# Third attention of a gated four-layer stack: the stacked parts of the queries and keys go through DRAM, and the first tile's maxima are turned in halves

## The chip, the cores and the metric

The kernel runs on one core of a Trainium2 chip. The metric is the device time of one execution in microseconds (us): 1753.15 is the median of three executions (1750.42 to 1754.8). One more execution was recorded by the profiler; the rows below all come from it.

## The reference, cut to what matters

The model has four layers over x of 32 x 64 x 256. Each adds a gated cross-attention-like block and a gated feed-forward block. The change touches only the fourth layer's first block (called the third attention here):

```
scores = einsum('bhtc,bhsc->bhts', rotary(split_heads(Wq x + bq)), rotary(split_heads(Wk c + bk))) / sqrt(8)
out = einsum('bhts,bhsc->bhtc', softmax(scores), split_heads(Wv c + bv))
x = x + tanh(g_xattn[3]) * (Wo out + bo)
```

x is read here as 32 batches of 64 channels by 256 positions; there are 8 heads of 8 channels. So each batch and head has a 256 x 256 matrix of scores over only 8 channels.

## The kernel before, in words

The eight blocks of the model run one after another on all engines. Each engine has its own program, written by hand, in loops over blocks of four tiles; engines wait for one another by semaphores. PE is TensorE, DVE VectorE, ACT ScalarE, POOL GpSimd, SP the sync engine that issues transfers.

In the third attention a tile is two batches: 128 partitions are 2 batches (k) x 64 channels, and there are 16 tiles. The scores must be as exact as float32, but their matmuls run in bf16. So a rotated query or key row is split by POOL into three bf16 parts that sum to it (`split`, lines 2160 to 2163: four operations for the queries, z = 0, and four for the keys, z = 1). The product is then the sum over six pairs of parts, `PAIRS3`. To have these six sums in one matmul, the parts are stacked: 6 pairs x 8 channels are 48 rows per batch, `MROW`. In the parts a partition is a channel of a head (64 per batch); in the stacks `qS` and `kS` a partition is a pair and one of 8 channels, and the heads lie beside one another (8 x 256 elements). That change of layout is done by transfers within the on-chip memory: SP issues at line 2131, for each z, batch and pair, one transfer of 64 rows of 512 bytes. That is 24 issues per tile, which all add to `stack_in`.

With the stacks there, PE makes scores twice. `largest` (line 1956) has queries on the partitions, and DVE takes row maxima (line 2224, 16 per tile). The negated maxima are split in two bf16 parts (`split_largest`, lines 2234 and 2235, per half of the heads), turned by PE (line 1965), copied by ACT (line 2075) and sent by ACT (line 2078, two transfers per half) as rows 48 and 49 of `qS`. `scores` (line 1977) then makes the transposed scores over 50 rows, with the maxima already taken off; ACT exponentiates (line 2098) and PE multiplies by the values (line 1991).

What sets the order: tile n does for each head h the scores and exponentials of tile n, one small step, the value product of the head before, and two units of `largest` of tile n + 1. The small steps are, for h = 0 to 7, those in `STEPS3` = (0, 7, 2, 1, 3, 5, 4, 6). Step 0 projects the queries of tile n + 2 (line 1942), step 2 its keys; DVE rotates them (lines 2203 and 2208), POOL splits them, SP stacks them. So a stack has about one tile of time from its projection to its first use: PE waits for `stack_in` of tile n + 1 at the first `largest` of tile n. POOL's split of a tile waits until the whole stack before it has landed, since there is one buffer of parts. In the second tile of each block of four DVE also makes the next block's layer norm (`normalise`, 21 small operations and eight larger ones). The last of the SP work is line 2338, the output of 2048 KB to DRAM.

The first tile has no tile before it: its stacks, all 16 maxima units, the split and the turn of both halves' maxima stand before the first scores.

Of the kernel before, what the change touches and what calls it, by code (L numbers as in the profile page):

```python
# [5 lines left out]
BF16 = mybir.dt.bfloat16  # L6
# [6 lines left out]
P = 128  # L13
BATCH, SEQ, DIM = 32, 64, 256
# [18 lines left out]
H3, D3 = 8, 8  # L33
# [27 lines left out]
def flamingo_kernel(nc, a, out):  # L61
    ctx = ExitStack()
    with ctx:
# [3 lines left out]
        def sem(name):  # L67
            return ctx.enter_context(nc.semaphore(name))
# [54 lines left out]
        def updated(ph, b):  # L123

            return BLOCKS * ph + b + 1
# [215 lines left out]
        z, at = part(work, at, [P, 2, BTOK])  # L341
# [844 lines left out]
        def bf_bank(i):  # L1186
            return bank[i].bitcast(BF16)
# [626 lines left out]
        C3 = DIM  # L1814
        PAIRS3 = ((0, 0), (0, 1), (0, 2), (1, 0), (1, 1), (2, 0))

        MROW = len(PAIRS3) * D3
        HALF = H3 // 2
        VW3 = SEQ
# [13 lines left out]
        parts3, at = part(work, at, [P, 3, 2, C3], BF16)  # L1833
# [18 lines left out]
        assert at <= 5632, at  # L1852
        vv3 = (vv0, vv1)

        a3_in = sem("a3_in")
        bd_zero = sem("bd_zero")
        vv_clear = sem("vv_clear")
        cs_ready = sem("cs_ready")
# [6 lines left out]
        stack_in = sem("stack_in")  # L1865
# [45 lines left out]
        def has_step(n, step):  # L1911
            if not isinstance(n, int):
                return True
            ahead = (2, None, 2, None, None, 1, 1, 0)[step]
            return n >= 1 if ahead is None else n + ahead < TILES
# [10 lines left out]
        def stack_rows(k, rows):  # L1926
            return slice(k * SEQ, k * SEQ + rows)

        def attn3_tensor(pe, ph):
# [16 lines left out]
            def largest(m, i, units):  # L1946

                if units[0] == 0:
                    pe.wait_ge(stack_in, 16 * STACK_DMAS * (m + 1))
                for u in units:  # L1950
                    k, tc, hp = u % 2, u // 2 % 2, u // 4
                    rows = stack_rows(k, MROW)
                    if u >= 2 or not isinstance(m, int) or m >= 1:
                        pe.wait_ge(mx_read, 16 * m + u - 1)
                    for h in range(2):
                        ins = nc.tensor.matmul(bank[u % 2][:, h * C3:(h + 1) * C3],  # L1956
                                               qS[rows, i, 2 * hp + h, tc * P:(tc + 1) * P], kS[rows, i, 2 * hp + h, :],
                                               start=True, stop=True)
                    ins.then_inc(s1_done, 1)

            def turn_largest(m, half, used):
                pe.wait_ge(m_ready, 2 * m + half + 1)
                pe.wait_ge(misc_read, used)
                for tc in range(2):
                    ins = nc.tensor.transpose(bf_bank(7)[0:4 * HALF, tc * P:(tc + 1) * P],
                                              mm3[:, half, tc, :, :, :].rearrange("p k s h -> p (k s h)"), ident_h[:, :])
                ins.then_inc(m_turned, 1)

            def scores(n, i, h):
# [4 lines left out]
                for sc_ in range(2):  # L1974
                    for k in range(2):
                        rows = stack_rows(k, MROW + 2)
                        ins = nc.tensor.matmul(bank[2 + 2 * (h % 2) + k][:, sc_ * C3:(sc_ + 1) * C3],  # L1977
# [76 lines left out]
            project(0, 0, 2, 2)  # L2054
            project(1, 1, 0, 3)
            project(1, 1, 1, 4)
            largest(0, 0, range(16))
            turn_largest(0, 0, 5)
            for t in range(BT):
                tile_(0, t)  # L2060
            with pe.Fori(1, BLOCKS - 1) as b:
# [8 lines left out]
        def attn3_scalar(act, link, ph):  # L2070
            def largest(m, i, half, used):
# [5 lines left out]
                for k in range(2):  # L2077
                    act.dma_start(qS[k * SEQ + MROW:k * SEQ + MROW + 2, i, half * HALF:(half + 1) * HALF, :],
                                  mT3[2 * k * HALF:2 * (k + 1) * HALF, half, :]).then_inc(mrow_in[half], 16)
# [36 lines left out]
            outputs(TILES - 1)  # L2116
            turned(TILES - 1)

        STACK_DMAS = 4 * len(PAIRS3)

        def attn3_dmas(sp, ph):
            def stack(m, i):

                for z, stacks in enumerate((qS, kS)):
                    sp.wait_ge(parts_ready, 2 * m + z + 1)
                    for k in range(2):
                        for c, parts in enumerate(PAIRS3):
                            rows = slice(k * SEQ + c * D3, k * SEQ + (c + 1) * D3)  # L2130
                            sp.dma_start(stacks[rows, i, :, :],  # L2131
                                         parts3[k * SEQ:(k + 1) * SEQ, parts[z], z, :]).then_inc(stack_in, 16)

            def tile_(b, t):
                n = BT * b + t
                if has_step(n, 0):
                    stack(n + 2, (t + 2) % BT)

            sp.wait_ge(vv_clear, 1)
            stack(0, 0)  # L2140
            stack(1, 1)
            for t in range(BT):
                tile_(0, t)
            with sp.Fori(1, BLOCKS - 1) as b:
                for t in range(BT):
                    tile_(b, t)
            for t in range(BT):
                tile_(BLOCKS - 1, t)

        def attn3_gpsimd(pool, link, ph):  # L2150
            def split(m):

                if not isinstance(m, int) or m >= 1:

                    pool.wait_ge(stack_in, 16 * STACK_DMAS * m)
                one = ones[:, 0:1].broadcast_to([P, C3])
                for z in range(2):
                    pool.wait_ge(rot_ready, 2 * m + z + 1)
                    p = [parts3[:, s, z, :] for s in range(3)]
                    link(nc.gpsimd.tensor_tensor(p[0], rot3[:, z, :], one, ALU.mult))  # L2160
                    link(nc.gpsimd.tensor_tensor(rest3[:, z, :], rot3[:, z, :], p[0], ALU.subtract))
                    link(nc.gpsimd.tensor_tensor(p[1], rest3[:, z, :], one, ALU.mult))
                    nc.gpsimd.tensor_tensor(p[2], rest3[:, z, :], p[1], ALU.subtract).then_inc(parts_ready, 1)

            def contexts(b):
                nc.gpsimd.tensor_tensor(cs3, ctx_nat[:, bass.ds(BT * b, BT), :],
                                        ones[:, 0:1].unsqueeze(2).broadcast_to([P, BT, C3]), ALU.mult).then_inc(cs_ready, 1)

            def tile_(b, t):
                n = BT * b + t  # L2170
                if has_step(n, 0):
                    split(n + 2)
                if t == BT - 2 and has_step(n, 0):
                    pool.wait_ge(p3_v, BT * b + BT)
                    contexts(b + 1)

            pool.wait_ge(x_done, updated(ph, 0))
            pool.wait_ge(ctx_in, 16)
            contexts(0)
            split(0)  # L2180
            split(1)
            clear_values(link, 1).then_inc(vv_clear, 1)
            for t in range(BT):
                tile_(0, t)
            with pool.Fori(1, BLOCKS - 1) as b:
                link.enter(b - 1, 6 * BT)
                for t in range(BT):
                    tile_(b, t)
            link.leave(BLOCKS - 2)
            for t in range(BT):  # L2190
                tile_(BLOCKS - 1, t)

        def attn3_vector(dve, link, ph):
# [26 lines left out]
            def largest(m, units):  # L2220
                for u in units:
                    k, tc, hp = u % 2, u // 2 % 2, u // 4
                    dve.wait_ge(s1_done, 16 * m + u + 1)
                    nc.vector.tensor_reduce(out=mx3[:, tc, k, 2 * hp:2 * hp + 2],  # L2224
                                            in_=bank[u % 2].rearrange("p (h s) -> p h s", h=2), axis=AX,
                                            op=ALU.max).then_inc(mx_read, 1)

            def split_largest(m, half):

                dve.wait_ge(mx_read, 16 * m + 8 * half + 8)  # L2230
                if not isinstance(m, int) or m >= 1:
                    dve.wait_ge(m_turned, 2 * m + half - 1)
                mx, mm = mx3[:, :, :, half * HALF:(half + 1) * HALF], mm3[:, half, :, :, :, :]
                link(nc.vector.tensor_scalar(mm[:, :, :, 0, :], mx, -1.0, None, ALU.mult))
                nc.vector.scalar_tensor_tensor(out=mm[:, :, :, 1, :], in0=mx, scalar=-1.0, in1=mm[:, :, :, 0, :],
                                               op0=ALU.mult, op1=ALU.subtract).then_inc(m_ready, 1)
                dve.wait_ge(m_ready, 2 * m + half + 1)
# [55 lines left out]
            values(0, 0)  # L2293
            rotate(1, 0, p3_q)
            rotate(1, 1, p3_k)
            largest(0, range(16))
            split_largest(0, 0)
            split_largest(0, 1)
            for t in range(BT):
                tile_(0, t)  # L2300
            with dve.Fori(1, BLOCKS - 1) as b:
# [183 lines left out]
```

## Time and profile before

| | us |
|---|---|
| median of the executions shown | 1753.15 |
| the profiled execution | 1745.52 |
| its span, first to last instruction | 1743.7 |
| third attention, first issue of a stack (1178.18) to the last tile's first `largest` (1528.14) | 349.96 |

Busy in the span: PE 1290.4 us (74%), DVE 1066.2 (61%), ACT 455.2 (26%), POOL 306.9 (18%). "SPq" is SP's queue of transfer issues, and its time is no busy time of the table. The share of an engine over the whole span says little on this change: the eight stages have different limits, and only the stage from 1178 us on is touched. The granted TensorE clock (PEclk) is in parts of full speed.

### The profile page before, as it was taken

How to read it: one execution, taken by the hardware profiler on the slowest of the kernel's cores; microseconds unless marked ns; L12 is line 12 of the kernel's file. 1: busy time of each engine (PE TensorE's matmuls, PEld its weight loads, DVE VectorE, ACT ScalarE, POOL GpSimd, SP SyncE). 2: the span in 40 equal slices, each digit the busy share in tenths (PEclk: the TensorE clock that was granted, in tenths of full speed). 3: DMA queues.
4: the chain of work that ended last, by engine and by line, in shares of the span. 5: the costliest groups of instructions: out<-in, count | busy, mean ns of one | idle time of the engine just before them, and what ended most of it. 6: DMA issues, size and time to landing. Idle time of an engine off the chain costs nothing.

```text
span 1743.7 us, 20441 instructions
## 1 busy us (share of the span) xinstructions
PE 1290.4 (74%) x6664; PEld 725.4 (42%) x6670; DVE 1066.2 (61%) x2575; ACT 455.2 (26%) x632; POOL 306.9 (18%) x287
## 2 busy tenths in 40 slices
PE   0011899999979989957767445545888888899997
PEld 0010544444434456635544222222444444455554
DVE  8988434454353356557767788874778777742222
ACT  1124222222113133322222122211444434351110
POOL 2111000000013500022344222233132222200000
PEclk9995899999989999988898566675899999999999
DMA  9000000002000010011110000001111111100001
GB/s 301 12 13 11 1 0 0 0 0 100 0 19 0 0 61 0 1 25 25 24 24 0 19 1 0 0 0 37 38 38 39 39 37 37 38 2 1 0 0 48
DMA packets 65554, 43.16 MB, mean 25 GB/s; under 512 B 25040, under 2 KB 61776, under 8 KB 65232
## 3 DMA queue, kind: packets, MB, share of 16 engines
q1 hardware_dynamic: 64848, 42.09, 8.4%
q8 instruction: 33, 0.54, 0.1%
q14 instruction: 33, 0.27, 0.1%
q10 hardware_dynamic: 640, 0.26, 0.1%
HBM read 27.39 MB, written 2.10 MB: 17 GB/s over the span
## 4 chain that ended last, share of the span: by engine, by line
PE 49%; DVE 19%; issue 12%; SPq 9%; POOL 5%; ACT 2%; DMA 2%; DVEq 0%; POOLq 0%; ACTq 0%
SPq L2131 9%; PE banks L1004 6%; PE banks L406 5%; PE banks L623 5%; PE banks L402 5%; PE banks L837 3%; PE banks L1011 3%; POOL sb_work L1429 3%; PE banks L829 3%; PE banks L413 2%; PE banks L417 2%; DMA sb_work<-sb_work 2%; PE banks L1991 2%; DVE sb_work L317 2%; PE banks L1622 1%
## 5 line engine op out<-in xcount | busy, mean ns | idle before, releaser
L2224 DVE TENSOR_REDUCE sb_work<-banks 128x2 f32<-128x512 f32 x256 | 164.2, 685 | 68.5 <-PE banks L1956 64.3
L2098 ACT ACTIVATE sb_work<-banks 128x1024 f32<-128x1024 f32 x128 | 130.7, 1023 | 178.4 <-PE banks L1977 178.2
L523 DVE TENSOR_TENSOR sb_work<-sb_work,banks 128x512 f32<-128x512 f32 x72 | 49.4, 686 | 123.6 <-ACT sb_work L490 123.6
L1004 PE MATMUL banks<-sb_work,sb_shelf 128*128 128x512 f32 x256 | 114.4, 592 | 0.0
L1429 POOL TENSOR_TENSOR sb_work<-sb_work,sb_consts 128x512 f32<-128x512 f32 x64 | 66.4, 1067 | 265.7 <-ACT sb_work L1377 232.9
L1956 PE MATMUL banks<-sb_work 48*128 48x256 bf16 x512 | 65.4, 297 | 51.8 <-DMA sb_work<-sb_work 40.1
L406 PE MATMUL banks<-sb_work,sb_shelf 128*128 128x512 f32 (+1 forms) x192 | 92.2, 630 | 8.6 <-DVE sb_work L566 8.6
L623 PE MATMUL banks<-sb_work,sb_ctx_nat 128*64 128x512 f32 (+15 forms) x512 | 89.8, 510 | 7.8 <-DVE sb_work L685 7.8
L490 ACT ACTIVATE sb_work<-banks 128x512 f32<-128x512 f32 x72 | 42.9, 596 | 181.6 <-PE banks L402 116.2
L1083 DVE TENSOR_TENSOR sb_work<-sb_work,banks 128x512 f32<-128x512 f32 x32 | 22.0, 688 | 109.9 <-ACT sb_work L1069 109.9
L980 POOL TENSOR_TENSOR sb_late<-sb_w2n 128x1024 f32<-128x1024 f32 x10 | 22.7, 2268 | 371.6 <-DVE sb_work L677 370.9
L402 PE MATMUL banks<-sb_work,sb_shelf 128*128 128x512 f32 (+1 forms) x192 | 84.9, 593 | 0.0
L1991 PE MATMUL banks<-sb_work,sb_late 128*64 128x256 f32 x512 | 76.9, 425 | 0.2
L230 PE MATMUL banks<-sb_ident,sb_work 128*128 128x128 f32 x32 | 7.9, 427 | 92.6 <-DVE sb_work L319 92.6
L1991 PE MATMUL banks<-sb_work,sb_shelf 128*64 128x256 f32 x512 | 70.3, 396 | 0.0
L1004 PEld LDWEIGHTS banks<-sb_work,sb_shelf 128*128 128x128 f32 x256 | 48.6, 190 | 49.2 <-issue 47.8
L837 PE MATMUL banks<-sb_wpr,sb_work 128*128 128x256 f32 x256 | 61.6, 387 | 6.9 <-DVE sb_work L916 6.9
L1956 PEld LDWEIGHTS banks<-sb_work 48*128 48x128 bf16 x512 | 18.4, 96 | 114.1 <-issue 44.1
L829 PE MATMUL banks<-sb_work,sb_wgu 128*128 128x512 f16 x256 | 61.8, 388 | 2.5 <-DVE sb_work L898 2.5
L1639 PE MATMUL banks<-sb_ident_h,sb_work 128*128 128x128 bf16 x128 | 16.2, 305 | 62.9 <-DVE sb_work L1760 62.9
L623 PEld LDWEIGHTS banks<-sb_work,sb_ctx_nat 128*64 128x64 f32 x512 | 36.6, 136 | 60.1 <-issue 44.4
L1719 POOL TENSOR_TENSOR sb_work<-sb_work 128x512 f32<-128x512 f32 x32 | 40.2, 1266 | 118.5 <-ACT sb_work L1684 118.4
(285 smaller groups left out, 2599.4 us busy)
## 6 DMA issues: line engine op xcount, KB each, us to landing
sb_work<-sb_work SPq DMA_DIRECT2D x384, 32.0 KB
sb_work<-ctx_t SPq DMA_DIRECT2D x16, 256.0 KB, 4.4
sb_work<-ctx_t SPq DMA_DIRECT2D x4, 512.0 KB, 3.7
sb_ctx_nat<-ctx SPq DMA_DIRECT2D x1, 2048.0 KB, 11.0
sb_raw<-wguT SPq DMA_DIRECT2D x1, 2048.0 KB, 15.4
out<-sb_x SPq DMA_DIRECT2D x1, 2048.0 KB, 7.5
sb_x<-x SPq DMA_DIRECT2D x1, 1536.0 KB, 10.7
sb_raw<-wpT SPq DMA_DIRECT2D x1, 1024.0 KB, 13.4
```

Of the source, the lines that this page charges most:

```text
L402: ins = nc.tensor.matmul(dst[0:ms, :], w[:, c, m0:m0 + ms], moe_xT[:, c, :], start=c == 0, stop=c == KC - 1, skip_group_check=True)
L406: ins = nc.tensor.matmul(dst[0:ms, :], w[:, m0:m0 + ms], zz[:, k, :], start=False, stop=True, skip_group_check=True)
L623: ins = nc.tensor.matmul(o, ctx_nat[:, tap, g * SEQ:(g + 1) * SEQ], xg[:, g, :, l0 + 1 + 2 * tap:SEQ + 1 + 2 * tap], start=tap == TILES - ...
L829: ins = nc.tensor.matmul(bank[2 * (m % 2) + half], wgu[:, c, half * FF1 + m * P:half * FF1 + (m + 1) * P], xs[:, c, :], start=c == 0 and n ...
L837: ins = nc.tensor.matmul(bank[4 + t // 2][:, (t % 2) * DIM:(t % 2 + 1) * DIM], h1[:, m % 4, t * P:(t + 1) * P], wpr[:, m, :], start=m == 0 ...
L1004: ins = nc.tensor.matmul(bank[2 * (m % 2) + half], w[:, c, m * P:(m + 1) * P], xT3[:, c, :], start=c == 0, stop=c == KC - 1)
L1429: ins = nc.gpsimd.tensor_tensor(km_[:, hf, k, :, :], keys.unsqueeze(1).broadcast_to([P, 8, SEQ]), hm2.unsqueeze(2).broadcast_to([P, 8, SEQ ...
L1956: ins = nc.tensor.matmul(bank[u % 2][:, h * C3:(h + 1) * C3], qS[rows, i, 2 * hp + h, tc * P:(tc + 1) * P], kS[rows, i, 2 * hp + h, :], st ...
L1991: ins = nc.tensor.matmul(bank[6][k * SEQ:(k + 1) * SEQ, u * C3:(u + 1) * C3], vv3[j][:, sc_, 2 * k + u, a_ * VW3:(a_ + 1) * VW3], pt3[:, h ...
L2098: nc.scalar.activation(pt3[:, h % 2, :, :], o, ACT.Exp).then_inc(exp3, 1)
L2131: sp.dma_start(stacks[rows, i, :, :], parts3[k * SEQ:(k + 1) * SEQ, parts[z], z, :]).then_inc(stack_in, 16)
L2224: nc.vector.tensor_reduce(out=mx3[:, tc, k, 2 * hp:2 * hp + 2], in_=bank[u % 2].rearrange("p (h s) -> p h s", h=2), axis=AX, op=ALU.max).t ...
```

## The change

Each batch of three bf16 parts is written to a DRAM tensor `scratch`, already repeated as the pairs need it: `RUNS3` says that pairs 0 to 2 are written by one transfer, pairs 3 and 4 by a second, pair 5 by a third. For the queries one part is repeated over the pairs of a run; for the keys the parts 0 to n - 1 follow one another. Then SP waits until the three have landed (`parts_out`), and reads the stack back with one transfer per batch: 48 rows of 4096 bytes. So a tile has 10 issues, 6 out and 4 back, and two new waits on SP. POOL waits for `parts_out` too before it overwrites the parts.

Apart from that, the first tile's maxima are cut in two halves of 8 units: DVE splits the first half's after 8 units, and PE turns them before it goes on with the second 8.

```
+        RUNS3 = ((0, 3, 0), (3, 2, 1), (5, 1, 2))
...
+        scratch = nc.dram_tensor("scratch", (2, len(PAIRS3), 2, D3, H3, C3), BF16, kind="Internal").ap()
...
-            largest(0, 0, range(16))
+            largest(0, 0, range(8))
             turn_largest(0, 0, 5)
+            largest(0, 0, range(8, 16))
...
-        STACK_DMAS = 4 * len(PAIRS3)
+        STACK_DMAS = 4
...
                 for z, stacks in enumerate((qS, kS)):
                     sp.wait_ge(parts_ready, 2 * m + z + 1)
+                    for c0, n, s in RUNS3:
+                        src = parts3[:, s:s + 1, 0, :] if z == 0 else parts3[:, 0:n, 1, :]
+                        sp.dma_start(scratch[z, c0:c0 + n].rearrange("c k d h t -> (k d h) c t"),
+                                     src.broadcast_to([P, n, C3])).then_inc(parts_out, 16)
+                    sp.wait_ge(parts_out, 96 * m + 48 * z + 48)
                     for k in range(2):
-                        for c, parts in enumerate(PAIRS3):
-                            rows = slice(k * SEQ + c * D3, k * SEQ + (c + 1) * D3)
-                            sp.dma_start(stacks[rows, i, :, :],
-                                         parts3[k * SEQ:(k + 1) * SEQ, parts[z], z, :]).then_inc(stack_in, 16)
+                        sp.dma_start(stacks[k * SEQ:k * SEQ + MROW, i, :, :],
+                                     scratch[z, :, k].rearrange("c d h t -> c d (h t)")).then_inc(stack_in, 16)
...
+                    pool.wait_ge(parts_out, 96 * m)
                     pool.wait_ge(stack_in, 16 * STACK_DMAS * m)
...
-            largest(0, range(16))
-            split_largest(0, 0)
-            split_largest(0, 1)
+            for half in range(2):
+                largest(0, range(8 * half, 8 * half + 8))
+                split_largest(0, half)
```

On SP, the stage before began with the constants of this attention and then the stacks of the first six tiles in a row (144 issues; `REGISTER_ALU` and `ISA` are the loop's counters and waits):

```order
L1884 DMA sb_late<-w3T 64x64 x12
L1886 DMA sb_late<-b 64x5 x2
L1887 DMA sb_late<-rope 128x1024
L1889 DMA sb_late<-bv 128x64 x2
L2131 DMA sb_work<-sb_work 8x8x256 x144
```

Now the same place reads, for the two halves z of the first tile:

```order
L1893 DMA sb_late<-bv 128x64 x2
L2135 DMA scratch<-sb_work 128x3x256
L2135 DMA scratch<-sb_work 128x2x256
L2135 DMA scratch<-sb_work 128x256
L2139 DMA sb_work<-scratch 48x1x2048 x2
L2135 DMA scratch<-sb_work 128x3x256
L2135 DMA scratch<-sb_work 128x2x256
L2135 DMA scratch<-sb_work 128x256
L2139 DMA sb_work<-scratch 48x1x2048 x2
```

Twelve issues of 8 x 8 x 256 elements became three of 128 rows, a wait, and two of 48 rows.

On DVE, the maxima of the first tile stood before as one row of 16 with both halves' splits behind (2203 and 2208 are rotations, 2224 the maxima, 2234 and 2235 the split):

```order
L2203 SCALAR_TENSOR_TENSOR sb_work<-banks,sb_late 128x256 x2
L2208 TENSOR_TENSOR sb_work<-sb_work 128x256
L2224 TENSOR_REDUCE sb_work<-banks 128x2 x16
L2234 TENSOR_SCALAR sb_work<-sb_work 128x4x4
L2235 SCALAR_TENSOR_TENSOR sb_work<-sb_work 128x4x4
L2234 TENSOR_SCALAR sb_work<-sb_work 128x4x4
L2235 SCALAR_TENSOR_TENSOR sb_work<-sb_work 128x4x4
```

Now (lines 2233, 2243 and 2244 are the old 2224, 2234 and 2235):

```order
L2212 SCALAR_TENSOR_TENSOR sb_work<-banks,sb_late 128x256 x2
L2217 TENSOR_TENSOR sb_work<-sb_work 128x256
L2233 TENSOR_REDUCE sb_work<-banks 128x2 x8
L2243 TENSOR_SCALAR sb_work<-sb_work 128x4x4
L2244 SCALAR_TENSOR_TENSOR sb_work<-sb_work 128x4x4
L2233 TENSOR_REDUCE sb_work<-banks 128x2 x8
L2243 TENSOR_SCALAR sb_work<-sb_work 128x4x4
L2244 SCALAR_TENSOR_TENSOR sb_work<-sb_work 128x4x4
```

The first split moved ahead of the second eight maxima; every later tile is as it was.

## Rows read from the trace of the kernel before

**Rows 1.** The page, part 4: shares of the chain, by line.
```profile
SPq L2131 9%; PE banks L1004 6%; PE banks L406 5%; PE banks L623 5%; PE banks L402 5%; PE banks L837 3%; PE banks L1011 3%; POOL sb_work L1429 3%; PE banks L829 3%; PE banks L413 2%; PE banks L417 2%; DMA sb_work<-sb_work 2%; PE banks L1991 2%; DVE sb_work L317 2%; PE banks L1622 1%
```

**Rows 2.** Waits from 1178 to 1545 us: total us, times, longest.
```profile
POOL sb_work L2160 <- DMA sb_work<-sb_work: 81.0, 8, 14.8
...
PE banks L1956 <- DMA sb_work<-sb_work: 40.1, 12, 11.6
```

**Rows 3.** Busy us (x) of PE, PEld, DVE, ACT, POOL; PEclk; DMA; tile by tile.
```profile
1236.58:1262.06 25.48, 22.48 (x152) 11.54 (x153) 20.48 (x63) 8.97 (x11) 5.13 (x8) 0.80 0.13 33
...
1284.34:1305.12 20.78, 19.72 (x153) 10.40 (x153) 15.31 (x35) 9.56 (x12) 5.12 (x8) 0.88 0.16 39
...
1325.80:1349.34 23.54, 19.96 (x152) 10.42 (x153) 20.18 (x63) 8.97 (x11) 5.13 (x8) 0.93 0.14 35
...
1414.63:1439.50 24.87, 21.29 (x153) 10.97 (x154) 20.21 (x62) 8.97 (x11) 5.13 (x8) 0.86 0.13 33
...
1504.09:1528.14 24.05, 20.01 (x148) 9.75 (x149) 19.33 (x59) 8.85 (x11) 5.12 (x8) 0.86 0.14 34
sum 312.32, PE 267.91 PEld 140.60 DVE 236.93 ACT 132.77 POOL 77.50; mean PE 19.14 PEld 10.04 DVE 16.92 ACT 9.48 POOL 5.54
```

**Rows 4.** Timeline of PE, 1303 to 1326: start, us, line, [idle <-releaser].
```profile
1325.80 0.40 PE L1956 MATMUL banks<-sb_work 48*128 48x256 bf16 x4 [3.12 <-DMA sb_work<-sb_work]
```

**Rows 5.** Timeline of PE, 1365 to 1372.
```profile
1365.19 0.39 PE L1977 MATMUL banks<-sb_work 50*128 50x256 bf16 x4
...
1370.88 0.40 PE L1956 MATMUL banks<-sb_work 48*128 48x256 bf16 x4 [3.23 <-DMA sb_work<-sb_work]
```

**Rows 6.** Timeline of PE, 1284 to 1306, after a long wait.
```profile
1284.34 0.61 PE L1956 MATMUL banks<-sb_work 48*128 48x256 bf16 x4 [4.15 <-DMA sb_work<-sb_work]
...
1285.62 1.98 PE L1991 MATMUL banks<-sb_work,sb_late 128*64 128x256 f32 x8
...
1289.98 1.08 PE L1991 MATMUL banks<-sb_work,sb_late 128*64 128x256 f32 x8
...
1305.12 0.40 PE L1956 MATMUL banks<-sb_work 48*128 48x256 bf16 x4 [0.99 <-DMA sb_work<-sb_work]
```

**Rows 7.** Timeline of POOL, 1345 to 1372: the split of one tile.
```profile
1350.47 0.61 POOL L2160 TENSOR_TENSOR sb_work<-sb_work,sb_ones 128x256 bf16<-128x256 f32 x1 [13.83 <-DVE sb_work L2208]
...
1352.60 0.67 POOL L2163 TENSOR_TENSOR sb_work<-sb_work 128x256 bf16<-128x256 f32 x1
1355.11 0.61 POOL L2160 TENSOR_TENSOR sb_work<-sb_work,sb_ones 128x256 bf16<-128x256 f32 x1 [1.85 <-DVE sb_work L2208]
```

**Rows 8.** Line 2131 on SP: ns min/median/max of one issue.
```profile
L2131 SPq DMA_DIRECT2D sb_work<-sb_work x384: 599/613/1784, 1178.2 to 1523.7; - x192
```

**Rows 9.** Chain of waits, 1330 to 1350: the last landing of a stack.
```profile
1343.92 2.28 DMA sb_work<-sb_work
```

**Rows 10.** DMA issues: count, KB each, median us from issue to landing.
```profile
out<-sb_x SPq DMA_DIRECT2D x1, 2048.0 KB, 7.5
...
sb_late<-rope SPq DMA_DIRECT2D x1, 512.0 KB, 3.7
...
sb_late<-w3T SPq DMA_DIRECT2D x12, 16.0 KB, 2.0
```

**Rows 11.** Line 2338 on SP: ns of its issue.
```profile
L2338 SPq DMA_DIRECT2D out<-sb_x x1: 402/402/402, 1735.8 to 1735.8; - x1
```

**Rows 12.** Chain of waits, 1170 to 1216: the first tile.
```profile
1178.18 0.80 SPq L2131
...
1195.68 0.66 PE banks L1956 x4
...
1206.14 1.29 DVE sb_work L2224 x2
...
1209.90 2.10 DMA sb_work<-sb_work
```

**Rows 13.** Timeline of ACT, 1345 to 1372: the maxima's rows.
```profile
1360.76 1.31 ACTq L2078 DMA_DIRECT2D sb_work<-sb_work  x2
```

More of the change, by code:

```diff
@@ L1853, in flamingo_kernel @@
         vv3 = (vv0, vv1)
+        scratch = nc.dram_tensor("scratch", (2, len(PAIRS3), 2, D3, H3, C3), BF16, kind="Internal").ap()
         a3_in = sem("a3_in")
+        parts_out = sem("parts_out")
         bd_zero = sem("bd_zero")
```

## The prediction, made before the changed kernel was run

> **What bounds the kernel now.** Read first, in the page, the shares of the chain that ended last by line: SP's queue at line 2131, the issues of the stacks, has 9% of the span, more than any line of an engine [rows 1]. That is one line with 384 issues, so ask next who waited for it. The list of waits between 1178 and 1545 us gives two: PE's line 1956, the first `largest` of a tile, waited 40.1 us in 12 waits, and POOL's line 2160 81.0 us in 8 [rows 2]. Then cut the stage tile by tile, from each first `largest` to the next, and read the length, DVE's busy time and the clock of each [rows 3]. The 14 tiles from 1215.82 to 1528.14 take 312.32 us. Four of them hold a layer norm and take 25.48, 23.54, 24.87 and 24.05, together 97.94; the ten others take 214.38, so 21.44 each.
>
> What would a tile take if no stack were late? The timeline of PE tells it. The tile from 1305.12 ends at 1325.80, after 3.12 us of waiting for the transfer: 20.68 - 3.12 = 17.56 [rows 4]. The one from 1349.34 ends at 1370.88 after 3.23: 18.31 [rows 3, 5]. The tile from 1284.34 waited only 0.99 at its end, yet took 20.78 [rows 3, 6]. Look at its start: PE had been idle for 4.15 us, and the value product of eight matmuls that follows takes 1.98 instead of 1.08; it is at 1.08 again at 1289.98. The granted clock of that tile is 0.88 against 1.00 where there was no slow stretch. So a late stack costs twice: the wait, and some matmuls at 1.2 GHz instead of 2.4 after it. That is 0.9 from the product, 0.2 from each of four groups of scores (0.61 against 0.40 [rows 4, 6]) and about 0.5 from a projection, 2.2 us, my estimate; without it and the wait the tile takes 20.78 - 0.99 - 2.2 = 17.6. The layer-norm tile from 1325.80 ends with no stack late and has 20.18 us of DVE in 23.54 [rows 3]; it too began after a wait of 3.12 [rows 4], at clock 0.93, and 0.07 of its time is 1.6. It would take 21.9, and there DVE is the bound.
>
> Why the stack is late: POOL needs 1352.60 + 0.67 - 1350.47 = 2.80 us for one z [rows 7], 24 issues at 0.656 from start to start (0.613 and a gap) [rows 8] are 15.7, and the last one lands 2.28 after it is issued [rows 9]. Since POOL overwrites the parts only after that, the sum, 20.8 us, is the shortest time from stack to stack. It is longer than 17.6 or 18.3.
>
> **The change, part by part.**
>
> Removed: per tile 24 issues, 15.7 us of SP, on the path in the ten short tiles, hidden in the four with a layer norm.
>
> Added, per z: three issues of 128 rows. The trace has no such transfer out of the parts. The issue of the output took 0.40 [rows 11], a stack issue 0.61 [rows 8]; three cost 1.3 to 2.0. Then a wait for the landing in DRAM, call it W, from the end of the issue. From below: the output, 2048 KB, lands 7.5 after its issue, and the small load w3T of 16 KB 2.0 after its issue, of which the issue itself is 0.6 [rows 10], so 1.4 and at the very least 1.2. From above: the stack's own landing of 2.28 [rows 9], plus 0.6 for a third transfer that is still behind the first two: 2.9. I take W = 2.0, nearer the stack's landing, since the source is the same. Then two issues at 0.656, and for the last z a landing R of 2 x 192 KB in rows of 4096 bytes. The rope table, 512 KB in such rows, lands in 3.7 against 2.0 for 16 KB [rows 10]: 1.7 us for 128 rows, 0.21 per row if 16 engines take eight each. R is 1.4 + 0.6 = 2.0 if the 96 rows spread as widely; if they went over only six engines, 16 rows each, 3.4 us of data begun 0.65 before, it would be 4.1. I take 3.0, the middle.
>
> A rule that speaks against this change bears on R. The Trainium skill, page "DMA: Bandwidth & Descriptors", section on why a DMA increments its semaphore by 16, says that a transfer runs on the largest number of engines up to 16 that divides both sides' slowest dimension; 48 rows on one side and 6 pairs on the other would give 6. No row here shows it. By it the sum below would have R = 4.1, 1.1 us more per stack.
>
> The wait also blocks: SP is in order, so the keys' three issues stand behind the queries' landing in DRAM. Nothing else is queued there; the output comes after the stage. The first z's POOL work starts 1.13 after the tile's start (1350.47 - 1349.34) [rows 3, 7]. The chain from a tile's first `largest` to the next stack is then 1.13 + 2.80 + 2 x (3 issues + W + 2 issues) + R. With 5 issues at 0.656 (3.3) and W = 2.0 it is 3.93 + 10.6 + 3.0 = 17.5. The keys' own way is not longer: their parts are ready at 1355.11 + 2.80 - 1349.34 = 8.6, and SP is free for them at 3.93 + 5.3 = 9.2. With all at the lower ends (2.6 + 1.2 twice, R = 2.0) it is 13.5; with all at the upper (3.3 + 2.9 twice, R = 4.1) 20.4.
>
> 17.5 is as long as the 17.6 of the short tiles and under the 18.3, so the stack is just in time and PE's own order becomes the bound. What is late next: in the layer-norm tile DVE, elsewhere PE with its value products and DVE's maxima in turn. The 14 tiles are four with a norm at 21.9 (87.6), four like the one from 1349.34 at 18.3 (73.2) and six at 17.6 (105.6), together 266.4: 45.9 less than 312.3. As the stack is only just in time I leave 5 us in for short waits: -41.
>
> Start of the stage: the first issue is at 1178.18, the first `largest` at 1195.68 [rows 12]. Now the first stack is there at 1178.2 + 10.6 + 3.0 = 1191.8. The second follows POOL: 1191.9 + 2.8 + 10.6 + 3.0 = 1208.3, where the second tile's `largest` ran at 1215.82.
>
> Maxima in halves: from 1195.68 the 16 units took until 1207.4 [rows 12] at half clock, 0.73 each; with the split, turn and ACT's rows, landing 2.10 after 1209.90 [rows 12], the first scores came at 1212.0 and the next `largest` 3.8 later. Uncut, that would be 1191.8 + 16.3 + 3.8 = 1211.9, later than the stack's 1208.3. Cut, the rows of the first half travel while the second 8 units run: these start about 1.2 late, for PE waits for the split and turn before them, and end at 1191.8 + 11.8 + 1.2 = 1204.8, so 1204.8 + 3.8 = 1208.6. The two parts of the change need each other here. Together 1215.8 - 1208.6 = 7. POOL's added wait for `parts_out` is covered by that for `stack_in`, which comes later: nothing.
>
> Sum: -41 - 7 = -48. On the profiled execution's 1745.52 that gives 1697.5. That execution is 7.6 below the median of 1753.15; on the median, which is what will be measured, 1705.
>
> **The rivals.**
>
> The round trip through DRAM binds. With W and R at the upper ends a stack is there after 20.4. The short tiles take 20.4 (ten times 1.0 less), the four others lose about 0.5 each, the start gains 1 to 2: -14, 1739. For it: nothing in the trace goes out and comes back, and two waits stand in a row on SP for each z. Against it: all landings of small transfers are 1.3 to 2.3 after the issue [rows 9, 10].
>
> Slower than before: the same chain, each landing dearer than any row. It decides where the chain passes the 21.44 of the ten tiles now: 3.93 + 6.6 + 2W + R = 21.44, so 2W + R = 10.9. With W = 4.5 (DRAM behind 128 x 3 small rows) and R = 5 the chain is 24.5; ten tiles lose 3.1, the four others nothing, and the second stack comes 6.5 later than now (7.8 for each z, 2.8 for POOL, 5 for R, twice over): +37, 1790. Against it speaks the output, which writes 2048 KB in 7.5 all told [rows 10]; a W of 4.5 for 64 KB behind 320 KB has no like.
>
> The maxima's rows come late. ACT sends them from 1360.76 for 1.31 us, and they land 2.10 later [rows 12, 13], at 1364.2; the scores that need them run at 1365.19 [rows 5]. One us of slack. The read-back falls into this stretch with 4096-byte rows on the same engines, where there were 512-byte ones. If that holds the rows for 3 us, each tile waits 2: 28 of the gain go, 1733. Against it: they need only a few packets, and the transfers use 0.16 of the engines' time.
>
> **How the numbers follow.** The forecast, 1705, has 0.62; its own range is 1690 to 1722, from all waits gone to 1 us left per tile. DRAM binding has 0.20, the late maxima 0.11, slower 0.07. The range 1688 to 1742 takes in the second and third and leaves out the slower case and what lies below. Runs of this kernel tell 0.3%, 5 us, from no change: 1748 to 1758. Of the DRAM case a quarter lies in that or beyond: faster 0.88, same 0.05, slower 0.07.
>
> **What would show it.** SP's line 2135 with issues of 0.4 to 0.65 and a wait behind each three of about 2 us; landings of line 2139 of 2 to 4 us. PE's waits of the first `largest` for the transfer should fall from 40.1 us to under 10, the 14 tiles from 312.3 to about 271 with the norm tiles near 22, the clock in them near 1.0, POOL's line 2160 waiting for DVE rather than for the transfer. The first `largest` should start near 1191.8 and the second tile's near 1208.6. I am wrong if tiles without a norm stay above 20 us; then the chain of waits names SP and the scratch transfers (DRAM), or `scores` waiting for ACT's rows (the third rival).

## The result, and the profile after

| | before | changed |
|---|---|---|
| median, us | 1749.74 (6 runs, 1742.34 to 1754.8) | 1734.79 (6 runs, 1726.74 to 1737.55) |
| ratio | | 0.9914, 95% interval 0.9893 to 0.9935 |
| profiled execution, us | 1745.52 | 1737.16 |
| its span | 1743.7 | 1735.4 |
| 14 tiles, first maxima of the second tile to those of the last | 312.32 | 302.60 |
| POOL's first split to the second tile's first maxima | 1215.82 - 1175.24 = 40.6 | 1216.31 - 1176.95 = 39.4 |

The changed kernel is 0.86% faster, 15 us. I had forecast 48 us. The profiled pair differs by 8.4 us only: the profiled execution of the kernel before is among the shorter of its kind, that of the changed kernel among the longer. Of the 8.4, 9.7 are in the tiles and 1.2 at the start, and the stage begins 1.7 later.

The shares of the chain, in the page of the changed kernel (line numbers are up to 9 higher than before):

```profile
PE banks L1004 6%; PE banks L623 5%; PE banks L406 5%; PE banks L402 5%; DMA sb_work<-scratch 4%; DMA scratch<-sb_work 3%; PE banks L837 3%; PE banks L1011 3%; POOL sb_work L1429 3%; PE banks L829 3%; PE banks L413 2%; PE banks L417 2%; DVE sb_work L317 2%; PE banks L1622 1%; PE banks L1995 1%
```

SP's queue is gone from the head of the list of [rows 1]. Two kinds of landing came instead: the read back with 4% and the write out with 3%. The list of waits from 1178 to 1545 us answers [rows 2]:

```profile
POOL sb_work L2169 <- DMA sb_work<-scratch: 95.0, 10, 14.5
...
PE banks L1960 <- DMA sb_work<-scratch: 31.3, 11, 11.3
```

PE's wait for the stack fell from 40.1 to 31.3 us only; POOL's grew from 81.0 to 95.0. So the stack is still late. Tile by tile, with the columns of [rows 3]:

```profile
1235.42:1257.87 22.45, 19.46 (x152) 10.14 (x153) 20.40 (x63) 8.98 (x11) 5.14 (x8) 0.92 0.24 72
...
1278.92:1298.45 19.53, 17.52 (x152) 9.59 (x153) 15.54 (x35) 9.57 (x12) 5.14 (x8) 1.00 0.27 82
1298.45:1318.76 20.31, 17.41 (x153) 9.45 (x153) 15.55 (x35) 9.57 (x12) 5.15 (x8) 0.99 0.28 81
1318.76:1345.69 26.93, 22.62 (x153) 11.33 (x153) 20.30 (x62) 8.97 (x11) 5.14 (x8) 0.82 0.20 60
...
1412.10:1435.70 23.60, 20.36 (x155) 10.52 (x154) 20.20 (x63) 9.58 (x12) 5.14 (x8) 0.89 0.23 68
...
1494.50:1518.91 24.41, 21.51 (x148) 10.76 (x149) 19.57 (x59) 8.86 (x11) 5.14 (x8) 0.79 0.23 66
sum 302.60, PE 265.88 PEld 139.54 DVE 237.03 ACT 132.89 POOL 77.68; mean PE 18.99 PEld 9.97 DVE 16.93 ACT 9.49 POOL 5.55
```

The ten tiles without a norm fell from 21.44 to 20.5 on average ((302.60 - 22.45 - 26.93 - 23.60 - 24.41) / 10), and to 19.9 without the one of 26.43; not to 17.6 or 18.3. The tiles with a norm are near what they were (97.94 before, 97.39 now).

The tile from 1385.67 took 26.43 us, and 22.43 before. It holds the step from one round of the loop to the next, at which VectorE does nothing for 3.40 us and waits for nothing that the profile shows. That step is no work of the change: before it took 3.23. New in this tile are a wait of 1.96 us for the rows of the maxima (shown below, with the third rival) and slow stretches: the granted clock is 0.84 against 1.00 before.

Where is the time between the parts and the stack? In the chain of waits of the first tile (start us, us, what; a landing counts from the end of the last issue):

```profile
1180.86 1.80 DMA scratch<-sb_work
...
1185.44 5.06 DMA scratch<-sb_work
...
1191.28 5.70 DMA sb_work<-scratch
```

The first z lands in DRAM after 1.80 us, as forecast (W = 2.0). The second z needs 5.06. The last landing of the read back, R, needs 5.70, where I had taken 3.0 and had an upper end of 4.1. A later tile shows the same:

```profile
1267.20 5.93 DMA scratch<-sb_work
...
1273.92 4.96 DMA sb_work<-scratch
```

The issues were no surprise. A write took 0.48 us in the median and a read 0.73; the writes, as ns min/median/max:

```profile
L2135 SPq DMA_DIRECT2D scratch<-sb_work x96: 369/480/1729, 1179.9 to 1506.1; - x96
```

What the transfer engines move during the read back of the first keys (40 slices of 0.175 us from 1190.5 us):

```profile
GB/s 0 0 0 0 0 0 0 0 70 70 70 47 70 94 70 140 164 140 140 164 140 117 140 187 117 140 23 23 47 23 47 0 0 0 0 0 0 0 0 0
```

There is no slice over 187 GB/s, and the best stretch stays near 140 to 164. The output of the kernel before moves 2048 KB in 7.5 us [rows 10], 280 GB/s, waits at both ends included. That made me suspect that only a part of the engines carries the read back.

### The profile page after: what moved, and what is told of

The parts are those of the page before. It is cut to its first block, busy times and chain, and to the rows that moved or that the text cites. A ratio compares the mean times of both kernels' runs of the same rounds, so it can differ in the third digit from the quotient of the medians.

```text
span 1735.4 us, 20241 instructions
## 1 busy us (share of the span) xinstructions
PE 1288.0 (74%) x6664; PEld 724.3 (42%) x6670; DVE 1071.7 (62%) x2575; ACT 455.5 (26%) x632; POOL 307.6 (18%) x287
## 4 chain that ended last, share of the span: by engine, by line
PE 48%; DVE 19%; issue 13%; DMA 8%; POOL 6%; ACT 2%; SPq 2%; DVEq 0%; POOLq 0%; ACTq 0%
PE banks L1004 6%; PE banks L623 5%; PE banks L406 5%; PE banks L402 5%; DMA sb_work<-scratch 4%; DMA scratch<-sb_work 3%; PE banks L837 3%; PE banks L1011 3%; POOL sb_work L1429 3%; PE banks L829 3%; PE banks L413 2%; PE banks L417 2%; DVE sb_work L317 2%; PE banks L1622 1%; PE banks L1995 1%
## 5 line engine op out<-in xcount | busy, mean ns | idle before, releaser
L1960 PE MATMUL banks<-sb_work 48*128 48x256 bf16 x512 | 64.3, 295 | 41.2 <-DMA sb_work<-scratch 31.3
L1960 PEld LDWEIGHTS banks<-sb_work 48*128 48x128 bf16 x512 | 18.3, 96 | 102.3 <-DVE sb_work L2233 38.5
```

## The experiments

Each kernel was timed against the kernel before on the same chip, and the ratios are to it. One execution of each also left a trace.

**1. Only DRAM, without the halves.** The changed kernel with the first tile's maxima whole:

```
-            largest(0, 0, range(8))
+            largest(0, 0, range(16))
             turn_largest(0, 0, 5)
-            largest(0, 0, range(8, 16))
```

(and the same on VectorE.)

> The parts go through DRAM as in the changed kernel, the first tile's maxima are not cut in halves. If the halves are worth little because the second tile's stack (from the chain of waits of the changed kernel, 1216.3 us) sets the next step: 0 to 2 us slower than the changed kernel (scores of the first tile start some 4 us later, but the second stack comes when it comes). If the halves carry the gain: back to the time of the kernel before, 15 us slower than the changed one.

Measured: 1733.58 us, ratio 0.9913 (0.9882 to 0.9945), against 0.9914 with the halves. No difference that can be told: the gain that the medians show is from DRAM. The timeline of PE, with the first maxima, the first scores and then the second tile's first maxima, shows in this kernel

```profile
1200.48 0.61 PE L1960 MATMUL banks<-sb_work 48*128 48x256 bf16 x4 [10.65 <-DMA sb_work<-scratch]
...
1219.88 0.61 PE L1981 MATMUL banks<-sb_work 50*128 50x256 bf16 x4 [6.93 <-DMA sb_work<-sb_work]
...
1222.42 0.61 PE L1960 MATMUL banks<-sb_work 48*128 48x256 bf16 x4
```

and in the changed kernel

```profile
1197.03 0.61 PE L1960 MATMUL banks<-sb_work 48*128 48x256 bf16 x4 [11.28 <-DMA sb_work<-scratch]
...
1210.39 0.70 PE L1981 MATMUL banks<-sb_work 50*128 50x256 bf16 x4
...
1216.31 0.61 PE L1960 MATMUL banks<-sb_work 48*128 48x256 bf16 x4 [3.21 <-DMA sb_work<-scratch]
```

With the halves PE gets to the scores sooner and then waits 3.21 us for the stack. From the first maxima to the second tile's it is 19.28 us with the halves and 21.94 without, 2.7 us more, which is too little for these medians to tell. Before it was 20.14, so the way through DRAM alone makes this place slower. The scores wait 6.93 us here, for the rows of the maxima: these land 4.88 us after their issue, where it was 2.10 before [rows 12]. They are issued while SP issues the read back of the second stack, so the likely cause is that the two share transfer engines; that was not tried apart.

```profile
1214.95 4.88 DMA sb_work<-sb_work
```

**2. Eight engines for the read back.** The order of two letters in the changed kernel, so that the outermost dimension in DRAM is the 8 channels and not the 6 pairs:

```
-                                     scratch[z, :, k].rearrange("c d h t -> c d (h t)")
+                                     scratch[z, :, k].rearrange("c d h t -> d c (h t)")
```

Queries and keys are both stacked so, and a sum over 48 rows does not mind their order.

> Only the order of the 48 rows of a stack is changed, (channel, pair) instead of (pair, channel), for queries and keys alike; the read back then has 8 and not 6 as its outermost dimension on the DRAM side. Theory 1 (the 96 rows of 4096 bytes of a read back run over only as many transfer engines as divide both sides' outermost dimension, six): now eight engines, 12 rows each instead of 16; the last landing falls from about 5.6 us to 4.6 to 5.0, and the keys' landing in DRAM, which stands behind the queries' read back, from about 4.7 to 4; a stack comes 1 to 1.7 us sooner, ten short tiles gain that: 8 to 15 us faster than the changed kernel. Theory 2 (the landing is long because DRAM answers late, whatever the engines): no change within 4 us, landing stays at 5.6.

Measured: 1711.84 us, ratio 0.9783 (0.9758 to 0.9808): 23 us below the changed kernel, and the best of all. The same place in the chain:

```profile
1266.89 4.23 DMA scratch<-sb_work
...
1271.85 4.25 DMA sb_work<-scratch
```

The write went from 5.93 to 4.23, the last landing from 4.96 to 4.25 (5.70 to 4.24 in the first tile). The tiles:

```profile
1276.14:1293.96 17.82, 17.53 (x152) 9.61 (x153) 15.12 (x35) 9.29 (x13) 5.13 (x8) 1.00 0.31 90
...
sum 281.97, PE 259.42 PEld 137.36 DVE 237.22 ACT 132.54 POOL 77.50; mean PE 18.53 PEld 9.81 DVE 16.94 ACT 9.47 POOL 5.54
```

They sum to 281.97 instead of 302.60, and the 23 us are more than the 8 to 15 that I expected. The chain of a stack got 2.4 us shorter, and a stack that comes within the 18.4 us or so of a tile costs nothing: from the second tile on no wait of PE for a stack is over 0.75 us.

**3. All engines for the read back, at the price of more issues.** DRAM laid out per batch, so that both sides of a read are 48 adjoining rows:

```
+        scratch = nc.dram_tensor("scratch", (2, 2, len(PAIRS3), D3, H3, C3), BF16, kind="Internal").ap()
...
+                        for k in range(2):
+                            own = parts3[k * SEQ:(k + 1) * SEQ]
+                            src = own[:, s:s + 1, 0, :] if z == 0 else own[:, 0:n, 1, :]
+                            sp.dma_start(scratch[z, k, c0:c0 + n].rearrange("c d h t -> (d h) c t"),
+                                         src.broadcast_to([SEQ, n, C3])).then_inc(parts_out, 16)
...
+                                     scratch[z, k].rearrange("c d h t -> (c d) (h t)")).then_inc(stack_in, 16)
```

> The DRAM tensor is laid out per batch, so a stack of one batch is 48 adjoining rows on both sides (16 divides both); in exchange each write out is cut in two of 64 rows, six issues per z instead of three. Theory 1: all 16 engines read, 6 rows each: the last landing falls from about 5.6 to 2.5 to 3.2 us and the keys' landing in DRAM to about 2; the three more issues per z cost 1.4 us of SP each. The stack comes 1 to 2.5 us sooner, 10 to 25 us faster than the changed kernel. Theory 2: landing stays near 5.6, and the more issues make it 10 to 25 us slower than the changed kernel.

Measured: 1729.79 us, ratio 0.9883 (0.9859 to 0.9908), 5 us below the changed kernel where I had expected 10 to 25, and with intervals that overlap; 14 tiles in 295.75. The chain and the rate (slices of 0.125 us from 1193.5):

```profile
1273.86 1.89 DMA scratch<-sb_work
...
1276.12 3.50 DMA sb_work<-scratch
```

```profile
GB/s 0 49 168 45 0 0 0 0 0 0 0 0 0 0 164 164 66 164 492 295 361 426 164 295 131 164 229 33 0 0 0 0 0 0 0 0 0 0 0 0
```

The landing is 3.50 and the keys' write 1.89, and the rate reaches 492 GB/s in a slice. The landings are as theory 1 has them, or a little longer, and theory 2 fails. The time gained is small, as the six issues of 0.61 us per z take it back (three took 1.43 us in the changed kernel). The Trainium skill says how the engines are chosen (page "DMA: Bandwidth & Descriptors", section on why a DMA increments its semaphore by 16): the largest number up to 16 that divides both outermost dimensions. By it the three kernels use 6, 8 and 16. The traces agree: 5.70, 4.24 and 3.54 us in the first tile. No row names an engine, but the packets count them. The two reads of 48 rows are 96 packets of 4096 bytes, and beside them stand short ones:

```profile
DMA packets 108, 0.39 MB, mean 56 GB/s; under 512 B 12, under 2 KB 12, under 8 KB 108
DMA packets 112, 0.39 MB, mean 77 GB/s; under 512 B 16, under 2 KB 16, under 8 KB 112
DMA packets 208, 0.43 MB, mean 85 GB/s; under 512 B 48, under 2 KB 112, under 8 KB 208
```

The first line is the changed kernel (1190.5 to 1197.5 us), the second run 2 (1194.9 to 1200): 12 and 16 short packets for two transfers, 6 and 8 each. In the third, run 3 (1193.5 to 1198.5), the last write of 64 rows falls into the stretch, so it is 48 for three transfers, 16 each. These are the three numbers of the rule, if each engine adds one short packet per transfer. The order of the rows in DRAM also differs among the three kernels; what that adds was not tried apart.

**4. The floor.** The kernel before with one pair stacked of six, and ones in the rest:

```
-        STACK_DMAS = 4 * len(PAIRS3)
+        STACK_DMAS = 4
...
-                        for c, parts in enumerate(PAIRS3):
+                        for c, parts in enumerate(PAIRS3[:1]):
...
+            link(nc.vector.memset(qS, 1.0))
```

> The kernel before, but with only the first of the six pairs stacked (4 issues per tile instead of 24; the other 40 rows of every stack hold ones, set once by VectorE at the start of the stage, about 5 us). So no stack can be late. If my floor of a tile holds (17.6 to 18.3 us, 21.9 with a layer norm), the 14 tiles take 264 to 272 us instead of 312, no matmul in them runs at half clock for lack of work, and the whole is 40 to 50 us below the kernel before. Rival: the tiles are bound by PE and VectorE near 20 us anyway, and the 14 tiles take 290 or more: then the changed kernel could not have gained more than it did.

Measured: 1715.16 us, ratio 0.9817 (0.9786 to 0.9849). The tiles:

```profile
1253.64:1271.70 18.06, 17.87 (x155) 9.72 (x154) 15.53 (x37) 9.52 (x12) 7.03 (x9) 1.00 0.04 9
...
1308.24:1332.62 24.38, 20.27 (x155) 10.41 (x153) 21.14 (x65) 9.52 (x12) 5.13 (x8) 0.93 0.03 7
1332.62:1351.02 18.40, 17.86 (x155) 9.54 (x154) 15.47 (x36) 9.52 (x12) 7.03 (x9) 1.00 0.04 9
...
sum 286.71, PE 263.64 PEld 139.10 DVE 237.75 ACT 132.31 POOL 77.53; mean PE 18.83 PEld 9.94 DVE 16.98 ACT 9.45 POOL 5.54
```

The 14 tiles take 286.71, neither the 264 to 272 of the forecast nor quite the 290 of the rival. Most short tiles take 18.06 to 18.48 at full clock; one of 22.21 is again that at the step between rounds of the loop. The four with a norm take 98.3, as long as in the kernel before, though no stack is late. The timeline of PE in the second of them says why:

```profile
1323.44 0.39 PE L1956 MATMUL banks<-sb_work 48*128 48x256 bf16 x2 [2.09 <-DVE sb_work L2225]
...
1325.20 1.87 PE L1991 MATMUL banks<-sb_work,sb_late 128*64 128x256 f32 x8
```

PE waits for VectorE twice, 1.14 and then 2.09 us, and after that runs a value product at 1.87 instead of 1.08. So a tile with a norm can have a slow stretch without any late stack, behind the norm's own wait; here all four have one. But such a wait does not always bring one. In the kernel before, the tile with a norm from 1325.80 has the same wait of 2.09, and the product behind it takes 1.08; its slow stretch stands at its start, behind the wait of 3.12 for the stack:

```profile
1326.56 1.66 PE L1991 MATMUL banks<-sb_work,sb_late 128*64 128x256 f32 x8
...
1341.45 0.39 PE L1956 MATMUL banks<-sb_work 48*128 48x256 bf16 x2 [2.09 <-DVE sb_work L2224]
...
1343.22 1.08 PE L1991 MATMUL banks<-sb_work,sb_late 128*64 128x256 f32 x8
```

And one of the four in run 2 has no slow stretch at all:

```profile
1235.05:1257.55 22.50, 18.59 (x154) 9.90 (x152) 21.17 (x66) 9.51 (x12) 5.13 (x8) 1.00 0.24 72
```

So 286.71 is no floor to the last us either: run 2, in which all six pairs are still stacked, takes 281.97. Its ten tiles without a norm take 188.22 against 188.40 here; the whole difference is in the four with a norm, 93.75 against 98.31. The medians of the two runs, 1711.84 and 1715.16, cannot be told apart. The floor of the 14 tiles lies at 282 to 287.

**5. Both writes before either read.** The changed kernel, with SP's first wait moved behind the writes of both z:

```
-                    sp.wait_ge(parts_out, 96 * m + 48 * z + 48)
+                sp.wait_ge(parts_out, 96 * m + 96)
+                for z, stacks in enumerate((qS, kS)):
```

> As the changed kernel, but SP writes out the queries' and the keys' parts before it reads back either stack; the keys' writes so no longer stand behind the queries' read back on the same transfer engines. If that queue is why the keys' landing in DRAM takes 4 to 5 us against 1.8 of the queries', it falls to about 2 for both. The four read backs then stand in a row (32 rows on each of six engines): the last lands 8 to 9 us after its issue instead of 5.5. Sum within 2 us per stack of the changed kernel, so within 15 us of it. If the keys' landing stays at 4 to 5 us, something else delays it.

Measured: 1740.51 us, ratio 0.9966 (0.9944 to 0.9987), 6 us slower than the changed kernel by the medians and 9 by the ratios. The chain of the first tile:

```profile
1186.66 1.79 DMA scratch<-sb_work
...
1190.95 6.93 DMA sb_work<-scratch
```

The keys' write now lands after 1.79 as the queries' did, against 5.06 in the changed kernel. That it had stood behind the queries' read back is shown. The read back, four in a row, needs 6.93 in place of 5.70; I had expected 8 to 9. The scores here also wait for the rows of the maxima, seven times, 4.8 us together.

**6. Reading older data.** Two slots in DRAM, each tile reading what the tile before wrote, so that the parts are those of the wrong tile:

```
+                        sp.dma_start(scratch[i % 2, z, c0:c0 + n].rearrange("c k d h t -> (k d h) c t"),
...
+                                     scratch[(i + (not isinstance(m, int) or m >= 1)) % 2, z, :, k]
```

> As the changed kernel, but DRAM holds two slots, and every tile after the first reads back the slot that the tile before wrote (so the parts are of the wrong tile); same sizes and waits. Theory 1 (engines): the last landing of the read back stays at 5.0 to 5.7 us, same time as the changed kernel within 5 us. Theory 3 (DRAM answers late because the rows were written just before): the landing falls by 1 us or more, the kernel is 8 us or more faster.

Measured: 1732.28 us, ratio 0.989 (0.9856 to 0.9924). The last landings of two tiles:

```profile
1279.15 5.27 DMA sb_work<-scratch
...
1298.47 5.56 DMA sb_work<-scratch
```

They are as long as in the changed kernel. That the rows were written just before is not why they come late.

**7. Only the halves.** The kernel before with the first tile's maxima in halves (the lines that the first experiment took out), and no DRAM.

> The kernel before with only the first tile's maxima cut in halves; no DRAM. The second tile's first maxima wait for its stack, which 24 issues bring 20.1 us after the first tile's, whenever the scores come. Theory (the stack hides the halves): no change beyond 3 us; from the first tile's first maxima to the second's still 20 us, though the first scores start 3 to 4 us sooner after the first maxima (16.4 us before). Rival (the halves carry part of the gain by themselves): that distance falls to 16 or 17 us and the kernel is 3 to 4 us faster.

Measured: 1750.04 us, ratio 1.0008 (0.9993 to 1.0024). The first maxima, the first scores and the second tile's maxima:

```profile
1201.04 0.61 PE L1956 MATMUL banks<-sb_work 48*128 48x256 bf16 x4 [11.63 <-DMA sb_work<-sb_work]
...
1214.03 0.39 PE L1977 MATMUL banks<-sb_work 50*128 50x256 bf16 x1
...
1221.18 0.61 PE L1956 MATMUL banks<-sb_work 48*128 48x256 bf16 x4 [4.12 <-DMA sb_work<-sb_work]
```

The scores start 13.0 us after the maxima instead of 16.4, and PE then waits 4.12 for the stack: 20.14 us from tile to tile, exactly as before.

**8. Eight engines, without the halves.**

> As the run with rows ordered (channel, pair) for the eight-engine read back, but with the first tile's maxima not cut in halves. There the second tile's first maxima came 16.7 us after the first's, with the stack no longer far behind. Theory: now the scores decide, and that distance is 20 us: 2 to 4 us slower than with the halves. If the halves do nothing even here: distance under 18 us.

Measured: 1719.93 us, ratio 0.9826 (0.98 to 0.9852). The same three places in this kernel

```profile
1196.95 0.61 PE L1960 MATMUL banks<-sb_work 48*128 48x256 bf16 x4 [8.11 <-DMA sb_work<-scratch]
...
1214.18 0.61 PE L1981 MATMUL banks<-sb_work 50*128 50x256 bf16 x4 [4.75 <-DMA sb_work<-sb_work]
...
1216.72 0.61 PE L1960 MATMUL banks<-sb_work 48*128 48x256 bf16 x4
```

and with the halves:

```profile
1199.69 0.61 PE L1960 MATMUL banks<-sb_work 48*128 48x256 bf16 x4 [8.19 <-DMA sb_work<-scratch]
...
1212.73 0.39 PE L1981 MATMUL banks<-sb_work 50*128 50x256 bf16 x1
...
1216.39 0.61 PE L1960 MATMUL banks<-sb_work 48*128 48x256 bf16 x4 [0.64 <-DMA sb_work<-scratch]
```

19.77 against 16.70. With the stack sooner there, the halves are worth 3.1 us in the trace, as expected (2 to 4). The medians, 8 us apart, agree in sign, but their intervals just overlap.

## Why the prediction was right and wrong

The direction and the mechanism hold: the issues of SP bound ten of the tiles, the change took them away, and the first rival of the text, "the round trip through DRAM binds" with 1739, is what happened. Its sign came too: the tiles without a norm stayed above 20 us on average (20.5), with the scratch transfers in the chain of waits. The likeliest case had the gain at 48 us; 15 were measured. Two terms failed, and a third, the start, fell short.

*"R ... I take 3.0, the middle", and "W = 2.0" for both z.* R was 5.0 to 5.8 and the keys' W 1.8 to 5.9, over the upper ends I had written (4.1 and 2.9). For R I had the six engines as one end and took the middle; runs 2 and 3 show that the end was the case. At both ends my figure was 1.5 us or so too low (4.1 against 5.7 on six engines, 2.0 against 3.5 on all), which points to the base of 1.4 us, taken from a load of 16 KB. For W I wrote that the keys' issues stand behind the queries' landing, and did not see that their packets stand behind the queries' read back on the same transfer engines; run 5 shows it. The chain of a stack, forecast at 17.5, was 21.05 in the tile from 1257.87. Against run 4 this cost 302.60 - 286.71 = 15.9 us, against run 2 302.60 - 281.97 = 20.6, where I had allowed 5: 11 to 16 us of the miss.

*"The 14 tiles are four with a norm at 21.9, four ... at 18.3 and six at 17.6, together 266.4."* Without late stacks they take 282 to 287 (runs 2 and 4): 16 to 20 us of the miss, and which of the two terms was the larger stays open.

Of this, 6 to 11 us are the tiles with a norm, 23.4 (run 2) or 24.6 (run 4) on average and not 21.9. My working for the tile from 1325.80 was right: its slow stretch did come from the late stack, and the one tile without any took 22.50. But this was the shortest of four and the only one whose norm's own wait was followed by no slow stretch; I took it for all.

The other 9.5 us are the ten other tiles, 18.84 on average in run 4 and not 17.88. Eight take 18.06 to 18.48, and the 17.6 that I took for six of them is too low. Both numbers of 17.6 were from tiles that began after a wait for a stack. The changed kernel shows what such a start does, in its tiles at full clock. Four began after waits of 2.97, 1.94, 1.77 and 1.51 us, and without the wait at their end they took 17.57 to 17.61, the first of them 19.53 - 1.94:

```profile
1278.92 0.40 PE L1960 MATMUL banks<-sb_work 48*128 48x256 bf16 x4 [2.97 <-DMA sb_work<-scratch]
...
1298.45 0.40 PE L1960 MATMUL banks<-sb_work 48*128 48x256 bf16 x4 [1.94 <-DMA sb_work<-scratch]
```

Three began after none and took 18.08 to 18.45 (21.05 - 2.97 is the first). Run 4, where no tile begins after such a wait, has none under 18.06. That the other engines catch up in the wait is my reading and was not tried apart. The other two of the ten are the first (19.70) and the one with the step between rounds of the loop (22.21).

*The start, "together 7".* 1.2 us came. The second stack was there at 1216.31, not 1208.3, since it came 19.3 us after the first and not 16.5, and the first, 20.1 us after POOL began, was hardly sooner than before (20.4). "The two parts of the change need each other here" holds: the halves are worth nothing in the kernel before (run 7), 2.7 us in the trace of the changed kernel (run 1), where without them this place would be slower than before, and 3.1 us where the stack comes sooner (run 8 against run 2).

*The maxima's rows late*, the third rival: seen. Without the halves it costs most, 6.93 us of waiting in run 1. In the changed kernel one of them, at 1409,

```profile
1409.01 0.39 PE L1981 MATMUL banks<-sb_work 50*128 50x256 bf16 x4 [1.96 <-DMA sb_work<-sb_work]
```

waited 1.96 us, in the tile of 26.43; in all, such waits of the scores (weight loads counted too) are 4.4 us there, 8.1 before, all in the first tile, and none in run 2.

The slower case did not come. Added up: 31 us for the 14 tiles (16 to 20 of them for the tiles themselves, 11 to 16 for the stack) and 6 for the start are 37 of the 39.6 us between the forecast (48) and the profiled pair (8.4); the rest is time outside these stretches.

## What to carry to other kernels

Before a floor is read from a tile that ends in a wait, look at how it began: here a tile that also began after one came out 0.5 to 0.9 us too short (17.6 against 18.1 to 18.5). The floor is better had from a kernel in which the suspected transfer is cut to a fraction, and even that is one execution, in which slow stretches moved the sum by 5 us. And a transfer is priced by how many engines can share it and by what is queued behind it on these, not by its bytes and landing alone: here the order of two loops in one access pattern was worth more (23 us) than the whole change (15).

## What the runs showed of the hardware

- A read back of 2 x 192 KB in rows of 4096 bytes landed 5.70, 4.24 and 3.54 us after its last issue when the outermost sizes were 6, 8 and 48 in DRAM against 48 on chip, with 6, 8 and 16 short packets for each transfer.
- A write of 64 KB to DRAM behind 320 KB more landed 1.79 to 1.80 us after its issue when nothing was in front, sooner than the 2.28 from on-chip memory to on-chip memory [rows 9]; behind a read back on six engines it took 5.06, on eight 3.63; with reads on all engines and the write cut in two 1.89.
- Reading rows a tile old took as long (5.27 and 5.56 us, run 6) as reading rows written a few us before (5.0 to 5.8).
- The two small transfers of the maxima's rows landed 2.10 us after their issue with SP's stack transfers of 512-byte rows on the way, and 4.88 beside a read back in rows of 4096 bytes (run 1).
- After the same wait of 2.09 us inside a tile, a value product took 1.87 us in one tile (run 4) and 1.08 in another (kernel before).
